# Attention scores: the negated maxima as two more rows of the queries, sent by transfers, in place of matmuls that pick them

## The chip, the cores and the metric

The kernel runs on one core of one Trainium2 chip. The metric is device microseconds for one execution; a time is the median of some runs of the same program. PE is TensorE, PEld its weight loads, DVE VectorE, ACT ScalarE, POOL GpSimd, and SP the engine that issues most transfers (its queue is SPq in the trace).

## What is computed

A gray edge filter turns 8 images of 256 x 256 into 8 sequences of 256 rows by 256 features; then come an attention block of 16 heads of 16 features and a feed-forward block. Cut to what matters here:

```
h = edges(gray(x))                                     # (8, 256, 256)
q, k, v = (layernorm(h) @ W + b for each), q and k folded with Wp
scores = einsum('bnhi,bmhi->bnhm', q, k) / sqrt(D)     # D = 16
attn = softmax(scores, axis=-1)                        # exp(scores - max over m)
h = h + einsum('bnhm,bmhe->bnhe', attn, v)
h = h + 0.5 * feed-forward-like block of layernorm(h)
```

The step of interest is the subtraction of each query's maximum before the exponential.

## The kernel before

**Stages.** Four pairs of images pass through the edge filter, the normalisation and the query, key and value products (until about 102 us). Queries and keys are split into a high and a low part of their fp32 value, written to DRAM by `store_qk` and read back by `load_qk` in another layout: `qs` and `ks` hold, for each unit of two heads, 48 rows (three terms of 16 features) on partitions 0 to 47 for the first head and 64 to 111 for the second. Then comes attention (102 to 213 us), then the feed-forward block.

**Attention.** One step `s` (64 steps: 8 images, 8 units of two heads each) makes the scores of two heads of one image. The loop at the end of the TensorE program runs in rounds of two steps: `scores_by_query(s+10)` (L1209), `scores_by_key(s)` and `scores_by_key(s+1)` (L1232 and L1237), `scores_by_query(s+11)`, then `attend` (L1257), which multiplies finished exponentials with the values for four heads.

- `scores_by_query(k)`: four matmuls, scores with queries on the partitions, two banks of one ring of three banks. DVE's `largest` (L848) takes the negated maxima from them, one reduction per head, which frees the bank (semaphore `ring_freed`). It runs 10 steps ahead of the scores that use the maxima.
- After each four steps POOL splits the four units' maxima into a high and a low part (`split_max`), `neg` (L1267) transposes them into a bank of the same ring, and ACT copies them to `negrow` (`neg_rows`, L1054). `out` (L1275) transposes finished attention through the same ring; DVE scales it (L856, L859).
- `scores_by_key(s)`: the scores again, with keys on the partitions, in the banks `p2`. Since the maximum now lies along the free dimension, it is put into the bank first: two matmuls of 512 columns (L1232), whose stationary operand `pick` is a column of zeros and ones, spread one unit's row of `negrow` over all 128 partitions, and the four score matmuls (L1237) add to it. ACT's `exp_head` (L1047) then takes the exponentials.

**Where one waits.** `scores_by_key(0)` waits for `s_neg` (ACT has copied `negrow`), every fourth step likewise, and all steps wait for the exponentials two steps back. SP's program is one list in order: the stores of the last pair are issued by `store_qk(3, i)`, behind 24 loads of the pair before, and are followed by the loads of the feed-forward weights (`load_ffn`, L401 and L404).

The lines which the change turns on:

```
if u % 4 == 0:
    wait_drained(eng, ("neg", b, u // 4))
...
eng.matmul(p2[(n + v) % 4]..., pick[rows, u % 4:u % 4 + 1].broadcast_to([SPLIT, P]),
           negrow[rows, u // 4]..., start=True, stop=False)
```

Of the kernel before, what the change touches and what calls it, by code (L numbers as in the profile page):

```python
# [5 lines left out]
def vit_tower_kernel(nc, x, scharr, Wq, bq, Wk, bk, Wv, bv, Wp, ln_gamma, ln_beta,  # L6
# [13 lines left out]
    P = 128  # L20
# [15 lines left out]
    NCOL = HALF + SPLIT  # L36
# [46 lines left out]
    pick = at("pick", 18.5, [P, 4], fp32r)  # L83
    picked = at("picked", 18.5625, [P, 4], fp32)
    negrow = at("negrow", 18.75, [NCOL, 2, N], fp32r)
# [4 lines left out]
    negsplit = at("negsplit", 24.125, [P, NT, NCOL], fp32)  # L90
# [71 lines left out]
    with ctx:  # L162
# [22 lines left out]
        s_pick = sem("pick_ready")  # L185
# [183 lines left out]
        def _(eng):  # L369
# [20 lines left out]

            def stored(p, m):
                for i in (2 * m, 2 * m + 1):
                    eng.wait_ge(s_store[i], 32 * (p + 1))
# [27 lines left out]
            eng.dma_start(b2[:], fc2_bias.rearrange("(a n) -> a n", a=1).broadcast_to([P, E])).then_inc(s_small, 16)  # L421
            for b in range(4, B):
                load_x(b)
# [24 lines left out]
            for i in range(4):  # L448
                store_qk(3, i)

# [6 lines left out]
            for s in range(SLOTS):  # L457
                for p in (2, 3):
                    first = UNITS * (2 * p - 3) + 4
                    for m in range(KE):  # L460
                        k = s - first - 4 * m
                        if 0 <= k < 4:
                            if k == 0:
                                stored(p, m)
                            eng.wait_ge(s_p2, max(s, UNITS * (2 * p - 3) + 4 * (m + 1)))
                            for i in range(3 * k, 3 * k + 3):
                                load_qk(p, m, i)
                if s in (19, 20):
                    if s == 19:
                        eng.wait_ge(s_w1f, 2)  # L470
                    eng.wait_ge(s_p2, s)
                    load_ffn(1, 2 * s - 38)
                    load_ffn(1, 2 * s - 37)
# [10 lines left out]
        def _(eng):  # L484
# [35 lines left out]
            link(eng.memset(negsplit[:], 0.0))  # L520
# [24 lines left out]
            def split_max(b, half):  # L545
# [5 lines left out]
                hi, lo = ([negsplit[:, :, HALF * v + 4 * part:HALF * v + 4 * part + 4] for v in range(2)] for part in range(2))  # L551
# [138 lines left out]
        def _(eng):  # L690
# [66 lines left out]

            eng.wait_ge(s_ident, 1)
            link(eng.tensor_reduce(picked[:], ident[:].rearrange("p (v c r u) -> p u v c r", v=2, c=8, r=2)[:, :, :, 0], AX.XY, ALU.add))
            eng.tensor_copy(pick[:], picked[:]).then_inc(s_pick, 1)  # L760
# [219 lines left out]
        def _(eng):  # L980
# [68 lines left out]
            def neg_rows(b, half):  # L1049
                key = ("neg", b, half)  # L1050
                wait_entry(eng, key)
                if b >= 1:
                    eng.wait_ge(s_p2, UNITS * (b - 1) + 4 * (half + 1))
                eng.activation(negrow[:, half], entry_bank(key)[0:NCOL, 0:N], ACT.Copy).then_inc(s_neg, 1)  # L1054

# [79 lines left out]
        def _(eng):  # L1135
# [78 lines left out]
            def scores_by_key(s):  # L1214
# [3 lines left out]
                if s == 0:  # L1218
                    eng.wait_ge(s_pick, 1)

                    wait_drained(eng, [key for key in entries[:in_a] if ebank[key] == 3][-1])
                if u % 4 == 0:
                    wait_drained(eng, ("neg", b, u // 4))
# [6 lines left out]
                for v in range(2):  # L1230
                    rows = slice(HALF * v, HALF * v + SPLIT)
                    eng.matmul(p2[(n + v) % 4][:, :].rearrange("p (t n) -> p t n", t=NT), pick[rows, u % 4:u % 4 + 1].broadcast_to([SPLIT, P]),  # L1232
                               negrow[rows, u // 4].unsqueeze(1).broadcast_to([SPLIT, NT, N]), start=True, stop=False)
                for t in range(NT):
                    for v in range(2):
                        rows = slice(HALF * v, HALF * v + SPLIT)
                        ins = eng.matmul(p2[(n + v) % 4][:, t * N:(t + 1) * N], ks[rows, r, u, c + t * P:c + (t + 1) * P],  # L1237
                                         qs[rows, r, u, c:c + N], start=False, stop=t == NT - 1)
                ins.then_inc(s_p2, 1)

            def attend(G, t):
                b, g = G // 4, G % 4
                if t == 0:
# [4 lines left out]
                    if G == 0:  # L1248
                        eng.wait_ge(s_zero, 4)
# [12 lines left out]
            def neg(b, half):  # L1262
# [3 lines left out]
                for t in range(NT):  # L1266
                    ins = eng.transpose(entry_bank(key)[0:NCOL, t * P:(t + 1) * P], negsplit[:, t], ident[:])  # L1267
# [164 lines left out]
```

## Time and profile before

| | |
|---|---|
| median of 3 runs | 308.85 us (308.3 to 309.14) |
| profiled execution | 308.78 us, its span 307.0 us |
| PE busy | 286.5 us of the span |
| PEld, DVE, ACT, POOL busy | 224.3, 213.6, 161.4, 132.1 us |
| exponentials (L1047) | 128 of 602 ns |
| maxima (L848) | 128 of 684 ns |
| picking matmuls (L1232) | 128 of 398 ns, in pairs beside each other |
| transfers | 35.30 MB, mean 115 GB/s |

The span is the time from the first to the last instruction; 1.78 us of the profiled execution lie around it. A matmul's duration in the trace includes its way through the array, so that matmuls overlap: what one costs is the distance of the starts.

### The profile page before, as it was taken

What the parts mean: (1) busy time and instruction counts of PE and PEld (TensorE: products, weight loads), DVE (VectorE), ACT (ScalarE), POOL (GpSimd) and SP (SyncE); (2) the same over time, 40 slices, a digit from 0 to 9 for tenths busy, and PEclk for the clock granted to TensorE, in tenths of its full rate; (3) what the DMA queues carried; (4) which work ended last, traced back from release to release, by engine and by line L of the source; (5) the groups of instructions that cost most, each with busy time, mean ns of one, the idle gap of its engine ahead of it and who ended that gap; (6) DMA issues with size and microseconds to landing.
All of it is one profiled execution on the core that took longest, in us unless ns stands there. A gap on an engine that the chain in (4) does not pass through costs nothing.

```text
span 307.0 us, 6170 instructions
## 1 busy us (share of the span) xinstructions
PE 286.5 (93%) x2280; PEld 224.3 (73%) x2280; DVE 213.6 (70%) x423; ACT 161.4 (53%) x304; POOL 132.1 (43%) x250
## 2 busy tenths in 40 slices
PE   0499999999999999999999999898999999999996
PEld 0378878887677766666666666565898988989976
DVE  8978984785799988888889888634835734642332
ACT  1391453523333478768777876776344434434440
POOL 7605240330200018862859562066759489500000
DMA  6978019895398971678582000000000200200202
GB/s 211 324 191 270 2 69 288 181 217 206 108 281 252 326 270 55 183 185 270 162 174 76 4 3 2 0 2 2 0 1 2 69 2 0 68 2 0 70 0 68
DMA packets 26631, 35.30 MB, mean 115 GB/s; under 512 B 5082, under 2 KB 15594, under 8 KB 26602
## 3 DMA queue, kind: packets, MB, share of 16 engines
q1 hardware_dynamic: 26440, 34.77, 38.0%
q8 instruction: 18, 0.29, 0.4%
q10 hardware_dynamic: 162, 0.15, 0.1%
q14 instruction: 11, 0.09, 0.1%
HBM read 24.42 MB, written 10.49 MB: 114 GB/s over the span
## 4 chain that ended last, share of the span: by engine, by line
PE 81%; DVE 13%; ACT 3%; issue 2%; ACTq 0%; DVEq 0%
PE bank L1139 46%; PE bank L1257 9%; PE bank L1209 8%; PE bank L1232 4%; PE bank L1237 4%; DVE negmax L848 3%; PE bank L1275 3%; PE bank L1267 1%; DVE gray L725 1%; PE bank L1161 1%; PE bank L1283 1%; PE bank L1176 1%; DVE qk_l L838 1%; DVE gray L724 1%; DVE xn L813 1%
## 5 line engine op out<-in xcount | busy, mean ns | idle before, releaser
L848 DVE TENSOR_REDUCE negmax<-bank 128x2 f32<-128x512 f32 x128 | 82.0, 684 | 6.1 <-PE bank L1209 5.8
L1047 ACT ACTIVATE probs<-bank 128x512 f32<-128x512 f32 x128 | 66.1, 602 | 28.2 <-PE bank L1237 28.2
L902 DVE TENSOR_TENSOR y_l<-yf,y_h 128x512 fp32r<-128x512 f32 x32 | 23.7, 743 | 39.1 <-ACT yf L1073 39.0
L1070 ACT ACTIVATE y_h<-bank,b1col 128x512 fp32r<-128x512 f32 x32 | 22.1, 689 | 47.8 <-PE bank L1139 47.8
L1139 PE MATMUL bank<-w_h,y_h 128*128 128x256 f32 x128 | 36.9, 289 | 2.5 <-DVE y_l L902 2.1
L1139 PE MATMUL bank<-w_h,y_l 128*128 128x256 f32 x128 | 36.2, 282 | 0.0
L1139 PE MATMUL bank<-w_l,y_h 128*128 128x256 f32 x128 | 36.2, 282 | 0.0
L1257 PE MATMUL bank<-probs,vals 128*32 128x256 f32 x512 | 34.3, 385 | 0.0
L1209 PE MATMUL bank<-ks,qs 48*128 48x256 f32 x256 | 32.2, 329 | 1.3 <-DVE negmax L848 0.7
L1209 PEld LDWEIGHTS bank<-ks,qs 48*128 48x128 f32 x256 | 19.3, 184 | 15.7 <-DVE negmax L848 6.4
L1139 PEld LDWEIGHTS bank<-w_h,y_h 128*128 128x128 f32 x128 | 24.4, 190 | 4.6 <-DVE y_l L902 3.6
L1237 PEld LDWEIGHTS bank<-qs,ks 48*128 48x128 f32 x256 | 24.2, 184 | 2.7
L1232 PE MATMUL bank<-negrow,pick 48*128 48x512 f32 x128 | 25.8, 398 | 0.0
L1139 PE MATMUL bank<-nt_h,w_h 128*128 128x512 f32 x64 | 25.8, 402 | 0.0
L1237 PE MATMUL bank<-qs,ks 48*128 48x256 f32 x256 | 25.5, 277 | 0.0
L1139 PE MATMUL bank<-nt_h,w_l 128*128 128x512 f32 x64 | 25.3, 395 | 0.0
L1139 PE MATMUL bank<-nt_l,w_h 128*128 128x512 f32 x64 | 25.0, 390 | 0.0
L1139 PEld LDWEIGHTS bank<-w_h,y_l 128*128 128x128 f32 x128 | 24.4, 191 | 0.7
L1139 PEld LDWEIGHTS bank<-w_l,y_h 128*128 128x128 f32 x128 | 24.4, 190 | 0.0
L1073 ACT ACTIVATE yf<-bank,b1col 128x512 f32<-128x512 f32 x32 | 21.8, 682 | 1.4 <-DVE y_l L902 1.4
L553 POOL TENSOR_SCALAR negsplit<-negmax 128x8 fp32r<-128x8 f32 x32 | 5.9, 205 | 38.4 <-DVE negmax L848 35.4
L563 POOL TENSOR_TENSOR hid<-hid,att 128x256 f32<-128x256 f32 x16 | 12.1, 757 | 23.6 <-DVE att L859 23.5
(147 smaller groups left out, 612.6 us busy)
## 6 DMA issues: line engine op xcount, KB each, us to landing
xr<-in_x SPq DMA_DIRECT2D x8, 768.0 KB, 9.0
qs<-qk_parts SPq DMA_DIRECT2D x48, 128.0 KB, 3.3
ks<-qk_parts SPq DMA_DIRECT2D x48, 128.0 KB, 3.4
qk_parts<-qk_h SPq DMA_DIRECT2D x16, 256.0 KB, 3.2
qk_parts<-qk_l SPq DMA_DIRECT2D x16, 256.0 KB, 3.5
wraw<-in_L_ffn_fc_q SPq DMA_DIRECT2D x4, 512.0 KB, 4.6
wscale<-in_L_ffn_fc_scales SPq DMA_DIRECT2D x4, 512.0 KB, 6.7
out<-osb SPq DMA_DIRECT2D x16, 128.0 KB, 1.8
```

The source lines that it names most:

```text
L563: eng.tensor_tensor(h, h, att[:, u % 2, :], ALU.add).then_inc(s_h2, 1)
L848: eng.tensor_reduce(negmax[:, b % 2, u, v], entry_bank(key)[:, :].rearrange("p (t k) -> p t k", t=NT), AX.X, ALU.max, negate=True).then_in ...
L902: eng.tensor_tensor(y_l[:, p % 2, f], yf[:, n % 2], y_h[:, p % 2, f].bitcast(fp32), ALU.subtract).then_inc(s_y, 1)
L1047: eng.activation(probs[:, n % PBUF], p2[n % 4][:, :], ACT.Exp).then_inc(s_exp, 1)
L1070: eng.activation(y_h[:, p % 2, f], src, ACT.Silu, bias=b1col[:, f:f + 1])
L1073: eng.activation(yf[:, n % 2], src, ACT.Silu, bias=b1col[:, f:f + 1]).then_inc(s_silu, 1)
L1139: ins = eng.matmul(dst, l, r, start=first and i == 0, stop=i == len(steps) - 1 and not more_after)
L1209: ins = eng.matmul(entry_bank(("head", k, v))[:, t * N:(t + 1) * N], qs[rows, r, u, c + t * P:c + (t + 1) * P], ks[rows, r, u, c:c + N], s ...
L1232: eng.matmul(p2[(n + v) % 4][:, :].rearrange("p (t n) -> p t n", t=NT), pick[rows, u % 4:u % 4 + 1].broadcast_to([SPLIT, P]), negrow[rows, ...
L1237: ins = eng.matmul(p2[(n + v) % 4][:, t * N:(t + 1) * N], ks[rows, r, u, c + t * P:c + (t + 1) * P], qs[rows, r, u, c:c + N], start=False, ...
L1257: ins = eng.matmul(av[OROWS * j:OROWS * (j + 1), 0:N], vals[:, b, t, h * VW:h * VW + OROWS], probs[:, (4 * G + j) % PBUF, t * N:(t + 1) * ...
L1275: ins = eng.transpose(entry_bank(key)[:, g * P:(g + 1) * P], otr_of(4 * b + g)[:, t * P:(t + 1) * P], ident[:])
```

## The change

The maxima become two more rows of the contraction. `qs` gets on partitions 48 and 49 (and 112, 113) the high and the low part of the negated maxima; `ks` gets two rows of ones there. The score matmuls then contract over 50 rows and give score minus maximum by themselves, and the two picking matmuls of each step are gone. `scores_by_key` starts its bank itself.

The rows come by transfers: after ACT has copied the transposed maxima (now 16 rows in place of 112) to `negrow`, SP issues two transfers per half image (`pass_neg`), each of 2 x 4 x 256 elements, with the semaphores `neg_rows_loaded0` and `neg_rows_loaded1`; 16 half images make 32 transfers. `scores_by_key` waits for these and no longer for ACT's copy, and ACT's next copy waits for the transfers that read `negrow`. Four transfers fill the rows of ones from a small tile, in front of the loads of images 4 to 7. Two small DVE instructions that made `pick` are gone, and POOL clears a smaller tile.

```
@@ sync, helpers
+            def pass_neg(b, half):
+                wait_drained(eng, ("neg", b, half))
+                if b >= 4:
+                    eng.wait_ge(s_p2, UNITS * (b - 4) + 4 * (half + 1))
+                cols = slice((b % 2) * N, (b % 2 + 1) * N)
+                for v in range(2):
+                    row = HALF * v + SPLIT
+                    eng.dma_start(qs[row:row + 2, (b // 2) % 2, half * 4:(half + 1) * 4, cols].bitcast(fp32),
+                                  negrow[8 * v:8 * v + 8, half, :].bitcast(fp32)).then_inc(s_nld[half], 16)
@@ sync, before load_x(4)
+            eng.wait_ge(s_zero, 3)
+            for r in range(2):
+                for v in range(2):
+                    row = HALF * v + SPLIT
+                    eng.dma_start(ks[row:row + 2, r].rearrange("p u (c n) -> p (u c) n", n=P).bitcast(fp32),
+                                  ones[:].unsqueeze(1).broadcast_to([2, UNITS * COLS // P, P])).then_inc(s_ones, 16)
@@ sync, last pair
             for i in range(4):
                 store_qk(3, i)
+                if i == 1:
+                    pass_neg(0, 0)
+            pass_neg(0, 1)
@@ sync, attention
             for s in range(SLOTS):
+                if s >= 1 and neg_after(s - 1):
+                    pass_neg(*neg_after(s - 1))
@@ vector
-            eng.wait_ge(s_ident, 1)
-            link(eng.tensor_reduce(picked[:], ident[:].rearrange("p (v c r u) -> p u v c r", v=2, c=8, r=2)[:, :, :, 0], AX.XY, ALU.add))
-            eng.tensor_copy(pick[:], picked[:]).then_inc(s_pick, 1)
@@ scalar, neg_rows
                 if b >= 1:
-                    eng.wait_ge(s_p2, UNITS * (b - 1) + 4 * (half + 1))
-                eng.activation(negrow[:, half], entry_bank(key)[0:NCOL, 0:N], ACT.Copy).then_inc(s_neg, 1)
+                    eng.wait_ge(s_nld[half], 32 * b)
+                eng.activation(negrow[:, half], entry_bank(key)[0:16, 0:N], ACT.Copy).then_inc(s_neg, 1)
@@ tensor, scores_by_key
                 if s == 0:
-                    eng.wait_ge(s_pick, 1)
+                    eng.wait_ge(s_ones, 64)
...
                 if u % 4 == 0:
-                    wait_drained(eng, ("neg", b, u // 4))
+                    eng.wait_ge(s_nld[u // 4], 32 * (b + 1))
...
-                for v in range(2):
-                    rows = slice(HALF * v, HALF * v + SPLIT)
-                    eng.matmul(p2[(n + v) % 4][:, :].rearrange("p (t n) -> p t n", t=NT), pick[rows, u % 4:u % 4 + 1].broadcast_to([SPLIT, P]),
-                               negrow[rows, u // 4].unsqueeze(1).broadcast_to([SPLIT, NT, N]), start=True, stop=False)
                 for t in range(NT):
                     for v in range(2):
-                        rows = slice(HALF * v, HALF * v + SPLIT)
+                        rows = slice(HALF * v, HALF * v + KSTACK)
...
-                                         qs[rows, r, u, c:c + N], start=False, stop=t == NT - 1)
+                                         qs[rows, r, u, c:c + N], start=True, stop=True)
```

**Order on PE, the first round of attention.** Before, from `scores_by_query(10)` to `scores_by_query(11)`; the name in brackets is the semaphore waited for:

```order
L1209 MATMUL bank<-ks,qs 128x256 [waits ring_freed]
L1209 MATMUL bank<-ks,qs 128x256 x3
L1232 MATMUL bank<-negrow,pick 128x512 [waits neg_rows_copied,freed0,pick_ready]
L1232 MATMUL bank<-negrow,pick 128x512
L1237 MATMUL bank<-qs,ks 128x256 x4
L1232 MATMUL bank<-negrow,pick 128x512 [waits freed2,freed1]
L1232 MATMUL bank<-negrow,pick 128x512
L1237 MATMUL bank<-qs,ks 128x256 x4
L1209 MATMUL bank<-ks,qs 128x256 [waits ring_freed]
```

The same stretch of PE's list after the change (L1227 is the former L1209, L1251 the former L1237):

```order
L1227 MATMUL bank<-ks,qs 128x256 [waits ring_freed]
L1227 MATMUL bank<-ks,qs 128x256 x3
L1251 MATMUL bank<-qs,ks 128x256 [waits neg_rows_loaded0,freed0,neg_rows_copied,rows_of_ones_loaded]
L1251 MATMUL bank<-qs,ks 128x256 x3
L1251 MATMUL bank<-qs,ks 128x256 [waits freed2,freed1]
L1251 MATMUL bank<-qs,ks 128x256 x4
L1227 MATMUL bank<-ks,qs 128x256 [waits ring_freed]
```

The four picking matmuls are gone, and the first score matmul waits for a transfer.

**Order on SP, the end of the last pair.** Before, from the last loads of the pair before to the feed-forward weights:

```order
L389 DMA ks<-qk_parts 16x4x512 x6
L379 DMA qk_parts<-qk_h 128x512 [waits freed2]
L379 DMA qk_parts<-qk_l 128x512
L379 DMA qk_parts<-qk_h 128x512 [waits freed3]
L379 DMA qk_parts<-qk_l 128x512
L379 DMA qk_parts<-qk_h 128x512 [waits freed0]
L379 DMA qk_parts<-qk_l 128x512
L379 DMA qk_parts<-qk_h 128x512 [waits freed1]
L379 DMA qk_parts<-qk_l 128x512
L401 DMA wraw<-in_L_ffn_fc_q 128x1024 [waits qk_stored1,qk_stored0,filled2]
```

After, from the second store of that pair on:

```order
L379 DMA qk_parts<-qk_h 128x512 [waits freed3]
L379 DMA qk_parts<-qk_l 128x512
L399 DMA qs<-negrow 2x4x256 [waits neg_rows_copied]
L399 DMA qs<-negrow 2x4x256
L379 DMA qk_parts<-qk_h 128x512 [waits freed0]
L379 DMA qk_parts<-qk_l 128x512
L379 DMA qk_parts<-qk_h 128x512 [waits freed1]
L379 DMA qk_parts<-qk_l 128x512
L399 DMA qs<-negrow 2x4x256 [waits neg_rows_copied]
L399 DMA qs<-negrow 2x4x256
```

The first two transfers of maxima stand behind four stores and the next two behind all eight, in front of the feed-forward weights.

## Rows read from the trace of the kernel before

**Rows 1.** The page's chain that ended last, share of the span by line:

```profile
PE bank L1139 46%; PE bank L1257 9%; PE bank L1209 8%; PE bank L1232 4%; PE bank L1237 4%; DVE negmax L848 3%; PE bank L1275 3%; PE bank L1267 1%; DVE gray L725 1%; PE bank L1161 1%; PE bank L1283 1%; PE bank L1176 1%; DVE qk_l L838 1%; DVE gray L724 1%; DVE xn L813 1%
```

**Rows 2.** Timeline, a round: start us, us, engine, line, operation [idle before <-releaser]:

```profile
143.22 0.50 PE L1209 MATMUL bank<-ks,qs 48*128 48x256 f32 x4
143.56 0.40 PE L1232 MATMUL bank<-negrow,pick 48*128 48x512 f32 x2
143.83 0.69 DVE L848 TENSOR_REDUCE negmax<-bank 128x2 f32<-128x512 f32 x1 [0.24 <-PE bank L1209]
143.92 0.19 PEld L1232 LDWEIGHTS bank<-negrow,pick 48*128 48x128 f32 x2
144.03 0.39 PE L1232 MATMUL bank<-negrow,pick 48*128 48x512 f32 x2
144.26 0.40 PE L1237 MATMUL bank<-qs,ks 48*128 48x256 f32 x4
144.57 0.30 PEld L1209 LDWEIGHTS bank<-ks,qs 48*128 48x128 f32 x4
145.00 1.07 PE L1257 MATMUL bank<-probs,vals 128*32 128x256 f32 x16
```

**Rows 3.** Timeline, a round whose ring also carries an output:

```profile
151.34 0.40 PE L1237 MATMUL bank<-qs,ks 48*128 48x256 f32 x4
151.78 0.30 PEld L1209 LDWEIGHTS bank<-ks,qs 48*128 48x128 f32 x4 [0.25 <-DVE negmax L848]
```

**Rows 4.** An issue of SP; landing of the stores issued 101.1 and 101.6; landing of output stores:

```profile
102.10 0.73 SPq L379 DMA_DIRECT2D qk_parts<-qk_h  x1
...
DMA to landing us min/median/max: 3.2/3.4/3.6
...
out<-osb SPq DMA_DIRECT2D x16, 128.0 KB, 1.8
```

**Rows 5.** Timeline, weight loads of the first steps of attention:

```profile
102.09 0.19 PEld L1232 LDWEIGHTS bank<-negrow,pick 48*128 48x128 f32 x2
103.25 0.30 PEld L1209 LDWEIGHTS bank<-ks,qs 48*128 48x128 f32 x4 [0.15 <-DVE negmax L848]
108.10 0.19 PEld L1232 LDWEIGHTS bank<-negrow,pick 48*128 48x128 f32 x2
```

**Rows 6.** Landing of the stores issued from 104.0 to 104.7 us:

```profile
DMA to landing us min/median/max: 3.5/3.9/4.3
```

**Rows 7.** Timeline, rounds after the last maxima:

```profile
194.41 0.66 PE L1283 MATMUL bank<-ident,n 128*128 128x128 f32 x4 [0.87 <-ACT negrow L1054]
...
195.00 0.50 PE L1232 MATMUL bank<-negrow,pick 48*128 48x512 f32 x2
195.33 0.40 PE L1237 MATMUL bank<-qs,ks 48*128 48x256 f32 x4
195.77 2.07 ACT L1047 ACTIVATE probs<-bank 128x512 f32<-128x512 f32 x4 [1.41 <-PE bank L1237]
196.12 1.07 PE L1257 MATMUL bank<-probs,vals 128*32 128x256 f32 x16
197.71 0.50 PE L1232 MATMUL bank<-negrow,pick 48*128 48x512 f32 x2
```

**Rows 8.** Timeline, the start of DVE's gray sums:

```profile
8.87 0.18 DVE L759 TENSOR_REDUCE picked<-ident 128x4 f32<-128x16 f32 x1
9.16 0.87 DVE L724 SCALAR_TENSOR_TENSOR gray<-xr,gray 128x512 f32<-128x512 f32 x1
```

**Rows 9.** Landing of the images 4 to 7, issued at 17.3 to 20.5 us, and their first reader:

```profile
DMA to landing us min/median/max: 6.9/9.0/10.2
...
34.56 0.64 ACT L998 ACTIVATE gray<-xr 128x512 f32<-128x512 f32 x1
```

**Rows 10.** Chain in order of time: start us, us, work; the edge filter's first matmuls:

```profile
13.71 4.18 PE bank L1139 x9
...
21.04 2.09 PE bank L1139 x9
```

More of the change, by code:

```diff
@@ L35, in vit_tower_kernel @@
     HALF = P // 2
-    NCOL = HALF + SPLIT
+    KSTACK = SPLIT + 2
     UNITS = HEADS // 2
@@ L82, in vit_tower_kernel @@
     unused = at("unused", 18.375, [P, 1], fp32)
-    pick = at("pick", 18.5, [P, 4], fp32r)
-    picked = at("picked", 18.5625, [P, 4], fp32)
-    negrow = at("negrow", 18.75, [NCOL, 2, N], fp32r)
+    negrow = at("negrow", 18.75, [16, 2, N], fp32r)
     b2 = at("b2", 20.75, [P, E], fp32)
@@ L89, in vit_tower_kernel @@
     recip = at("recip", 24, [P, 2, HEADS], fp32)
-    negsplit = at("negsplit", 24.125, [P, NT, NCOL], fp32)
+    negsplit = at("negsplit", 24.125, [P, NT, 16], fp32)
+    ones = at("ones", 24.25, [2, P], fp32)
     vals = at("vals", 25, [P, B, NT, HEADS * VW + 16], fp32)
@@ L184, in vit_tower_kernel @@
         s_border = sem("gray_borders_zeroed")
-        s_pick = sem("pick_ready")
+        s_ones = sem("rows_of_ones_loaded")
+        s_nld = [sem("neg_rows_loaded0"), sem("neg_rows_loaded1")]
         s_band = sem("band_ready")
@@ L519, in _ @@
             link(eng.memset(mhalf[:], -0.5))
-            link(eng.memset(negsplit[:], 0.0))
+            eng.memset(ones[:], 1.0).then_inc(s_zero, 1)
             eng.memset(vals[:, :, :, 0:HEADS * VW].rearrange("p b t (h v) -> p (b t) h v", v=VW)[:, :, :, D:VW], 1.0).then_inc(s_zero, 1)
@@ L550, in split_max @@
                 src = negmax[:, b % 2, half * 4:(half + 1) * 4].rearrange("p u v t -> p v t u")
-                hi, lo = ([negsplit[:, :, HALF * v + 4 * part:HALF * v + 4 * part + 4] for v in range(2)] for part in range(2))
+                hi, lo = ([negsplit[:, :, 8 * v + 4 * part:8 * v + 4 * part + 4] for v in range(2)] for part in range(2))
                 for v in range(2):
@@ L1248, in attend @@
                     if G == 0:
-                        eng.wait_ge(s_zero, 4)
+                        eng.wait_ge(s_zero, 5)
                         wait_read(eng, last_turns[3])
@@ L1266, in neg @@
                 for t in range(NT):
-                    ins = eng.transpose(entry_bank(key)[0:NCOL, t * P:(t + 1) * P], negsplit[:, t], ident[:])
+                    ins = eng.transpose(entry_bank(key)[0:16, t * P:(t + 1) * P], negsplit[:, t], ident[:])
                 ins.then_inc(s_ent, 1)
```

## The prediction

> **What bounds the kernel now.** I read the page's busy shares first: PE is busy nearly throughout. The chain that ended last gives the line of the picking matmuls, L1232, 4% of the span, or some 12.9 us [rows 1]. The views that decide are the timelines of PE, its weight loads and DVE in single rounds, for they tell whether a pick delayed anything.
>
> Rows 2 show a round. The first query scores start at 143.22, the first pick 0.34 us later, a pick with its four score matmuls takes 0.47 (143.56 to 144.03), and `attend` starts at 145.00 and takes 1.00. DVE takes a maximum from 143.83 to 144.52, and only then is the bank free for the second query scores, whose weights are loaded at 144.57. Had they waited for nothing, that load would have stood where loads stand that are pulled ahead: 0.11 us ahead of the matmul's start (143.92 for the one of 144.03), so about 0.11 behind the last score matmul's start, at 144.37. So there were 0.20 us to spare: **DVE's first maximum, not the picks, sets the second query scores.** In a round that carries an output, DVE begins later and the spare time is larger: the load comes 0.44 behind the last score matmul's start and has DVE as its releaser [rows 3]. The rest of a round is query scores, `attend` and DVE's other maxima, none of which the change touches. After the last query scores (step 53) PE has no such wait, and a round is PE from end to end [rows 7].
>
> **The change part by part.**
>
> Picks in steps 0 to 53: two picks per step go, 0.47 − 0.24 = 0.23 us of a step, 0.46 of a round. The cover is DVE's maximum: PE reaches the second query scores 0.46 earlier and waits 0.46 longer. Gain 0. Bounds: none below 0; above, the most a round could gain is DVE's idle time of 0.24 [rows 2], 27 rounds, 6.5 us, if something that I take for DVE's pace were PE's. I take 0, since both spare times are positive.
>
> Picks in steps 54 to 63: five rounds. In rows 7 the pick starts at 195.00, the scores at 195.33, the exponentials at 195.77, `attend` at 196.12. Without picks the exponentials start 0.33 earlier and `attend` 0.46 earlier than now, counted from the round's start. The round took 2.71 (195.00 to 197.71) and would take 2.25. ACT needs for four exponentials 2.07 and for a copy of half the columns some 0.25 more (an estimate, half of one exponential's share), 2.3 in all, so it may hold back this shortest round by 0.05 to 0.1. The first of the five rounds gains only 0.33, as its end hangs on ACT: PE's next transposes, at 194.41, waited for ACT's copy of the last maxima [rows 7], which stands behind the exponentials. Sum 0.33 + 4 x 0.47 = 2.2 us, gained; bounds 1.2 (ACT sets all five, 5 x 0.23) and 2.3.
>
> The wait of step 0: now its first weight load stands at 102.09 and the second query scores of that round at 103.25 [rows 5]. Afterwards it needs the first two transfers. SP comes to them when it now issues the next store, at 102.10 [rows 4]; an issue takes about 0.5, so the second goes out at 102.6. In front of them are the stores issued at 101.1 and 101.6, which land after 3.2 and 3.6, the later at 105.2 [rows 4]. On quiet queues a transfer lands 1.8 after its issue [rows 4], which would be 104.4. I take 105.1, near the store, because these queues are full, with 104.4 and 106.9 (4.3 after issue, like the slowest in rows 6) as bounds. Then the scores load weights at 105.15; the second step follows 0.23 behind, and the second query scores at 105.15 + 0.11 + 0.23 + 0.11 = 105.6, against 103.25: a shift of **2.4 us**. It reaches everything behind, since PE waits in order and the maxima behind that stand in DVE's queue have no other work to fill the hole. Bounds 1.7 and 4.2.
>
> The wait of step 4: its weights load at 108.10 [rows 5], with the shift at 110.5. The second pair of transfers goes out behind the last two stores, which now issue at 104.0 and 104.7 and land within 4.3 [rows 6], the last at 109.0. With four more issues ahead the pair lands at 109.8 to 110.6. A delay of up to 0.66 there (0.20 + 0.46) is swallowed by the next wait for DVE. I take 0; if it lands like the slowest store it costs up to 1.
>
> Later transfers have two rounds, at least 2 x 2.78 = 5.6 us (a round of rows 2 goes from 143.22 to the end of `attend` at 146.00) [rows 2], for a copy that is read by SP, two issues and a landing of 3 to 4 [rows 4, 6]; the one for image 1 stands behind the feed-forward weights and has least to spare. I take 0. SP's own list grows by 32 issues of about 0.5, among loads that wait for PE's steps anyway.
>
> The rows of ones: four issues on SP and 256 KB in front of images 4 to 7. Those land 9.0 after issue, at most 10.2, so by 30.7, and the first is read at 34.56, when it had landed at about 24 [rows 9]. The ten microseconds between cover the four transfers. Cost 0.
>
> DVE's two instructions: 9.16 − 8.87 = 0.29 us in front of the gray sums [rows 8], which are the chain until PE begins. I take 0.25, gained, bounds 0 and 0.3.
>
> The two added rows (50 in place of 48) and 16 in place of 112 transposed rows: the number of columns streamed is the same. Within 0.1 either way.
>
> Sum: −0.25 + 2.4 − 2.2 = −0.05 us. The profiled execution took 308.78, the median is 308.85; the forecast on the scale of the median is **308.8 us**.
>
> The page "DMA: Bandwidth & Descriptors" of the Trainium skill, in "Why a DMA increments its semaphore by 16 and not by 1", says that a transfer is split over as many engines as divide both outermost dimensions. By it the 2 x 4 x 256 transfers would use two of sixteen, and land when those two have done with their part of the stores; no row here shows which two, so the bounds above stand.
>
> **The rivals.**
>
> *A longer hole, or a lower clock behind it (slower).* PE stands still from about 102.3 to 105.15. At the kernel's start nine matmuls took 4.18 us, later ones 2.09: the clock was at its lower level (1.2 GHz against 2.4) behind the idle start [rows 10]. If the hole brings it back for two to three rounds, their matmuls stretch from 2.23 us in a round (0.34 + 0.46 + 0.43 + 1.00) by a factor of 4.18 / 2.09 = 2 at most, to 3.5 if `attend` is bound by something else and to 4.5 if not, against 2.78 now, which costs 0.7 to 1.7 a round, so 1.4 to 5 us. It decides from the point where the hole is long enough to lower the clock; I price it at 2.3, near the lower end, since DVE's pace hides the first part. Without the clock, transfers that land like the slowest store make the hole 1.8 longer. Time: 308.8 + 2.3 = 311.1. The Trainium skill, "TensorE: Matmul & The Clock Gate", "HAM oscillation — how this bites in real kernels", warns that waits between bursts of matmuls return the array to its low clock; no row before the change has a hole like this one.
>
> *The transfers land soon (faster).* At 104.4 the shift is 1.7, the sum −0.75; with the picks gaining also a little beside the negated maxima's copy, −1.3: 307.5.
>
> *The picks were on the path in every round (faster).* The chain says so with 12.9 us. Against it stand the spare times. DVE's idle time limits it: −6.5, so 302.
>
> **How the numbers follow.** About 0.3% (0.9 us) is what a measurement can tell from no change. Forecast of balance, 0.50, its own range 307.9 to 309.8, of which 0.04 fall on either side beyond 0.3%; longer hole or lower clock 0.30; soon landed 0.14, of which 0.02 stay within; picks on the path 0.06. That gives faster 0.22, same 0.44, slower 0.34. Leaving out a tenth at each end, the range is 307.2 to 311.4.
>
> **What would show it.** Right: PE's first `scores_by_key` waits for a transfer for about 3 us at 102; rounds in the middle take as long as before, the one like rows 2 2.78 us; PE's weight loads of the second query scores now have DVE as releaser in nearly each round; the last five rounds are 2.2 us shorter; the feed-forward block starts where it did. Wrong: rounds shorter by some tenths; a second hole at step 4 or 8; score matmuls with starts twice as far apart behind the hole.

## The result, and the profile after

The changed kernel is slower: 320.04 us (317.92 to 322.93, 4 runs) against 308.87 (308.3 to 309.14, 4 runs), a ratio of 1.034, 95% interval 1.029 to 1.040. The forecast was 308.8 with 311.4 as its upper end, so the loss of 11.2 us lies far outside. Where the ratio of an experiment stands below beside its median, it leaves out executions in which the records show a longer spell at the lower clock.

The profiled execution took 317.92 us, its span is 316.2 us, 9.2 more than before. It was the fastest of the four; the others took 1.6 to 5.0 us more and have no trace, so the account below covers 9.2 us of the 11.2 between the medians. The page of the changed kernel, its row of the granted clock (40 slices of 7.9 us) and the head of its chain that ended last:

```profile
PEclk9999999999999599998799999999999999999999
...
PE 65%; DVE 21%; SPq 5%; issue 3%; DMA 3%; ACT 2%; ACTq 0%; DVEq 0%
PE bank L1157 42%; DVE negmax L866 8%; PE bank L1271 7%; PE bank L1227 6%; SPq L389 4%; DMA qs<-negrow 3%; PE bank L1251 3%; PE bank L1289 2%; DVE qk_l L856 2%; DVE gray L747 1%; PE bank L1179 1%; PE bank L1297 1%; DVE xn L831 1%; SPq L399 1%; DVE att L877 1%
```

Before, the clock stood at 9 in all 40 slices and neither SP nor a transfer of maxima was in the chain [rows 1]. Now the clock drops in two places, and SP's issues have 5% of the chain: the loads L389 4%, the new transfers L399 1%. The waits of PE by what ended them, then those of SP (us in total, times, longest):

```profile
PE bank L1227 <- DVE negmax L866: 9.8, 23, 0.7
PE bank L1251 <- DMA qs<-negrow: 9.4, 3, 5.3
...
SPq L399 <- ACT negrow L1072: 42.7, 9, 8.5
```

The first row answers to the spare time of [rows 2, 3]: PE now waits 0.7 at most for DVE, 23 times; that is where the picks' time went. The second row is where the loss begins: three waits for a transfer, 9.4 us, each with a price behind it. The third is SP, an engine with a list of its own, standing still in front of the new transfers, up to 8.5 us, with everything behind them in that list.

**The first wait (step 0).** Timeline, SP, PE's weight load and matmuls at the start of attention:

```profile
101.39 0.50 PE L1227 MATMUL bank<-ks,qs 48*128 48x256 f32 x4 [0.44 <-DVE negmax L866]
101.89 1.82 SPq L399 DMA_DIRECT2D qs<-negrow  x2
105.20 0.96 PEld L1251 LDWEIGHTS bank<-qs,ks 50*128 50x128 f32 x8 [3.52 <-issue]
105.23 1.01 PE L1251 MATMUL bank<-qs,ks 50*128 50x256 f32 x6 [3.34 <-DMA qs<-negrow]
```

Against [rows 5] (102.09) the weights load at 105.20. The clock of that stretch, from the windows (busy us and count by engine, then PEclk, DMA share, GB/s):

```profile
100.00:105.00 5.00, 1.46 (x13) 1.05 (x11) 3.29 (x7) 0.00 (x0) 0.00 (x0) 0.85 0.95 292
105.00:110.00 5.00, 4.77 (x32) 4.24 (x32) 1.75 (x3) 2.09 (x5) 0.72 (x4) 0.50 0.90 302
110.00:115.00 5.00, 4.54 (x58) 2.42 (x56) 4.33 (x8) 4.55 (x10) 0.00 (x0) 0.96 0.92 272
```

0.50 is the level of 1.2 GHz. DVE's maxima, compared by their starts in the two traces, stood 0.47 us earlier than before ahead of this place and 4.33 later behind it: a shift of 4.8 us.

**The second wait (step 24), not foreseen.** SP's issues around it, with ACT's copy that the pair of 145.60 sends, and PE's weight load and matmuls:

```profile
124.26 0.37 ACT L1072 ACTIVATE negrow<-bank 16x256 fp32r<-16x256 f32 x1
124.66 1.26 SPq L399 DMA_DIRECT2D qs<-negrow  x2
...
126.04 3.81 SPq L389 DMA_DIRECT2D qs<-qk_parts  x6
...
129.89 4.62 SPq L389 DMA_DIRECT2D ks<-qk_parts  x6
...
134.55 1.36 SPq L399 DMA_DIRECT2D qs<-negrow  x2
...
136.03 3.79 SPq L389 DMA_DIRECT2D qs<-qk_parts  x6
137.46 0.37 ACT L1072 ACTIVATE negrow<-bank 16x256 fp32r<-16x256 f32 x1
...
139.86 4.52 SPq L389 DMA_DIRECT2D ks<-qk_parts  x6
...
144.48 1.08 SPq L412 DMA_DIRECT2D wraw<-in_L_ffn_fc_q  x2
...
145.60 1.36 SPq L399 DMA_DIRECT2D qs<-negrow  x2
...
150.42 1.22 PE L1251 MATMUL bank<-qs,ks 50*128 50x256 f32 x8 [5.26 <-DMA qs<-negrow]
```

The same queue in the kernel before, from the first loads of image pair 2 to the weights of the second layer:

```profile
118.25 4.99 SPq L389 DMA_DIRECT2D qs<-qk_parts  x6
...
123.28 4.58 SPq L389 DMA_DIRECT2D ks<-qk_parts  x6
...
127.97 3.75 SPq L389 DMA_DIRECT2D qs<-qk_parts  x6
131.76 3.79 SPq L389 DMA_DIRECT2D ks<-qk_parts  x6
135.65 1.82 SPq L401 DMA_DIRECT2D wraw<-in_L_ffn_fc_q  x2
```

Read from below: the maxima for step 24 lay in `negrow` at 137.83, but SP sent them only at 145.60. From 126.04 to 144.38 it issues without a gap over 0.15: 24 loads in 16.7 us, 0.70 each, and one pair of transfers. With the first wait's shift alone the loads would have begun at 118.25 + 4.3 = 122.6; they begin at 126.04, because the pair in front of them (124.66) waits for ACT's copy of 124.26. So SP starts 3.4 late and has no slack to catch up. Then 1 MB of weights goes out at 144.48, one place ahead of the pair, which lands only at 150.4. DVE's maxima shift from 4.23 to 10.93 here: 6.7 us. The clock is low again:

```profile
148.00:154.00 6.00, 3.58 (x30) 2.08 (x30) 1.29 (x2) 2.07 (x5) 0.43 (x3) 0.50 0.73 248
154.00:160.00 6.00, 5.30 (x62) 3.66 (x66) 4.74 (x9) 4.50 (x10) 2.64 (x5) 0.94 0.01 3
```

**The third (step 40)** is short, PE waits 0.79 us, the shift grows by 0.4. **The tail** (steps 54 to 63) gives 2.0 back: the shift is 11.15 at the last maxima and the spans differ by 9.2. In sum −0.47 + 4.80 + 6.70 + 0.40 = 11.43, less 0.28 of small drifts 11.15, and 11.15 − 1.95 = 9.2.

### The profile page after: what moved, and what is told of

It reads as the page before. It is cut to its first block, busy times and chain, and to the rows that moved or that the text cites. A ratio compares the mean times of both kernels' runs of the same rounds, so it can differ in the third digit from the quotient of the medians.

```text
span 316.2 us, 5956 instructions
## 1 busy us (share of the span) xinstructions
PE 277.1 (88%) x2152; PEld 214.1 (68%) x2152; DVE 213.2 (67%) x421; ACT 162.5 (51%) x304; POOL 131.6 (42%) x250
## 4 chain that ended last, share of the span: by engine, by line
PE 65%; DVE 21%; SPq 5%; issue 3%; DMA 3%; ACT 2%; ACTq 0%; DVEq 0%
PE bank L1157 42%; DVE negmax L866 8%; PE bank L1271 7%; PE bank L1227 6%; SPq L389 4%; DMA qs<-negrow 3%; PE bank L1251 3%; PE bank L1289 2%; DVE qk_l L856 2%; DVE gray L747 1%; PE bank L1179 1%; PE bank L1297 1%; DVE xn L831 1%; SPq L399 1%; DVE att L877 1%
## 5 line engine op out<-in xcount | busy, mean ns | idle before, releaser
L1227 PE MATMUL bank<-ks,qs 48*128 48x256 f32 x256 | 33.0, 336 | 10.6 <-DVE negmax L866 9.8
L1227 PEld LDWEIGHTS bank<-ks,qs 48*128 48x128 f32 x256 | 20.2, 193 | 26.8 <-DVE negmax L866 16.4
L1271 PE MATMUL bank<-probs,vals 128*32 128x256 f32 x512 | 35.1, 393 | 0.0
L1251 PE MATMUL bank<-qs,ks 50*128 50x256 f32 x256 | 23.2, 301 | 9.4 <-DMA qs<-negrow 9.4
L1251 PEld LDWEIGHTS bank<-qs,ks 50*128 50x128 f32 x256 | 19.0, 201 | 11.5 <-DMA qs<-negrow 6.5
L1157 PE MATMUL bank<-gray_h,band_h 128*128 128x512 f32 x48 | 20.4, 425 | 0.7 <-DVE gray_l L752 0.7
```

The costliest lines, as they stand in the source:

```text
L1157: ins = eng.matmul(dst, l, r, start=first and i == 0, stop=i == len(steps) - 1 and not more_after)
L1227: ins = eng.matmul(entry_bank(("head", k, v))[:, t * N:(t + 1) * N], qs[rows, r, u, c + t * P:c + (t + 1) * P], ks[rows, r, u, c:c + N], s ...
L1271: ins = eng.matmul(av[OROWS * j:OROWS * (j + 1), 0:N], vals[:, b, t, h * VW:h * VW + OROWS], probs[:, (4 * G + j) % PBUF, t * N:(t + 1) * ...
```

## The experiments

Eleven kernels ran beside the two, one of them timed twice; all are below. "Shift" is how much later the maxima (or exponentials) of a step start than in the trace before. Experiments 2 to 6 and 8 are one execution each. The four of the changed kernel spread over 5 us, so these six are read from their traces, and their times are no more than a rough check.

**1. The picks taken out and nothing put in their place.**

```
-                for v in range(2):
-                    eng.matmul(p2[...], pick[...], negrow[...], start=True, stop=False)
...
-    ACT.Exp)
+    ACT.Exp, scale=0.01)
```

> The kernel before without its 128 picking matmuls, and nothing sent in their place: the maxima are still found, split, transposed and copied, but not subtracted (the exponential is taken of 0.01 times the score, at the same cost), so this part of the computation is left out. Theory 'the picks were hidden by DVE in steps 0 to 53': the exponentials of steps 0 to 52 start within 0.5 us of where they did, only the last five rounds gain, time 2.0 to 2.5 us under before, about 306.6. Rival 'the picks were on the path in every round', as the chain has it: 6 to 13 us under before. Rival 'a PE with less to do gets the lower clock': granted clock under 1.0 somewhere in attention, and no gain.

Measured: 306.77 us against 309.17, ratio 0.993 (0.991 to 0.996). In the trace the exponentials of steps 12 to 54 all keep one shift (−0.86 to −0.90, from an earlier start); it goes to −2.32 by step 62 and −2.5 in the span. PE's waits:

```profile
PE bank L1209 <- DVE negmax L848: 11.7, 28, 0.7
```

28 waits against 2 of 0.7 us in all before. So the picks of steps 0 to 53 were worth nothing and those of the tail 1.6 us (from −0.9 to −2.5); the change had no more than some 2 us to win. The granted clock stayed at 1.00, so the rival of a lower clock is out.

**2. The hole of step 0 in the kernel before.** PE also waits at step 0 until the second of the last pair's four stores (`s_store[1]`) has landed; no maxima are sent.

```
                     eng.wait_ge(s_pick, 1)
+                    eng.wait_ge(s_store[1], 32 * PAIRS)
```

> The kernel before with one wait added: PE's step 0 waits until the second half's key store of pair 3 has landed, near 105.2. Nothing else changes; it is the hole by itself. Theory 'a hole of 3 us lowers the clock for a while': granted clock 0.5 from about 103 to 110, step 2's exponentials 4.0 to 4.5 us later than before's, time 4 us over before. Rival 'the clock falls only together with the missing picks': clock 1.0, step 2 is 3 us late, time 3 us over.

Measured: 313.08 us, span 311.3. Timeline and windows:

```profile
104.25 0.80 PE L1233 MATMUL bank<-negrow,pick 48*128 48x512 f32 x2 [2.38 <-issue]
```

```profile
100.00:105.00 5.00, 2.20 (x16) 1.76 (x17) 3.25 (x7) 0.00 (x0) 0.00 (x0) 0.80 0.97 352
105.00:110.00 5.00, 5.00 (x36) 4.28 (x34) 1.88 (x3) 2.07 (x4) 0.72 (x4) 0.51 1.00 312
```

The shift goes from −0.50 to +4.32 and stays there to the end. A wait of 2.4 us at this place costs 4.8, with no transfer of maxima anywhere: about half of the price is what follows the hole, in which the granted clock is 0.51.

**3. The hole filled.** The changed kernel with 24 idle transposes on PE where it waits.

```
                 if s == 0:
+                    wait_read(eng, last_turns[3])
+                    keep_busy(24)
```

> The changed kernel with 24 idle transposes of the identity on PE (0.11 us each, 2.6 us) between the first query scores of attention and the wait of step 0. The hole is as long, but PE is busy in most of it. Theory 'the clock fell because PE stood still there, and that cost about 1.0 us': the granted clock stays at 1.0 until step 24, step 2's exponentials start 3.2 us after before's and not 4.2. Rival 'the clock fell for another reason': it falls as before and step 2 stays 4.2 late, or later by what the transposes take.

Measured: 317.38 us. PE at the hole, and a window behind it:

```profile
101.62 2.84 PE L1184 MATMUL bank<-ident 128*128 128x128 f32 x24 [0.29 <-DVE vals L849]
...
105.00:110.00 5.00, 4.89 (x56) 3.17 (x56) 3.86 (x6) 4.57 (x10) 0.72 (x4) 1.00 0.86 303
```

The clock is 1.00 from 100 to 115. The score matmuls start at 104.77, as long after the query scores in front of them as in the changed kernel (3.9 against 3.8), and the shift is 3.0 (−1.03 to +2.00) in place of 4.8: **the lower clock behind the first hole costs 1.8 us.** The hole at step 24 stays, 5.2 us.

**4. The first pair sent ahead of the loads of the pair before.**

```
             stored(1, 1)
+            pass_neg(0, 0)
             for k in range(12):
                 load_qk(1, 1, k)
...
-                if i == 1:
-                    pass_neg(0, 0)
```

> The changed kernel with the first two transfers of maxima issued in front of the 12 loads of pair 1's second half (near 92 us) instead of behind the second store of pair 3. Theory 'the hole at step 0 is SP's order and costs 3.2 us and 1.0 more by the clock': step 0's exponentials start at about 102.5, step 2's at most 3 us later, everything behind is 4.2 us earlier until step 22, and the hole at step 24 stays. Rival 'the rows of ones or something else holds step 0': no change at step 0. Rival 'the second pair of transfers takes over': a hole of 1 us or more at step 4.

Measured: 320.38 us. No hole at step 0 (shift −0.60), but at step 4, where PE waits 2.1 us for the second pair, and step 24 keeps 5.7 us. The place in SP's list makes the hole; moving one pair only uncovers the next, as the last rival said.

**5. The weights of the second layer two steps later.**

```
-                if s in (19, 20):
+                if s in (21, 22):
```

> The changed kernel with the second layer's weights loaded after steps 21 and 22 in place of 19 and 20, so that no megabyte stands in front of the maxima for step 24. Theory 'two causes for the hole at step 24, SP's late arrival and the weights in front': SP still issues these transfers near 144, they land about 3 us later, near 147, and the hole shrinks from 5.3 to 2 to 3 us; the low clock behind it is gone or shorter; time 3 to 4 us under the changed kernel. Rival 'only the weights in front': the hole goes wholly, 6 to 7 us under. Rival 'only SP's arrival': the hole stays at 5.

Measured: 322.69 us, a miss as a whole. Two parts of it lie away from step 24. Up to step 20 this is the changed kernel's own list, yet the first hole costs 6.6 us here in place of 4.8: the wait is 3.7 in place of 3.3, and the lower clock lasts until 114.7, 10.2 us in place of 6.8. The same kernel's hole thus has no fixed price, which may be a part of why its executions differ by 5 us; no trace shows the others. And the wait at step 40 grew from 0.8 to 1.8. At step 24 it tells what was asked:

```profile
147.09 1.35 SPq L399 DMA_DIRECT2D qs<-negrow  x2
148.55 0.93 SPq L412 DMA_DIRECT2D wraw<-in_L_ffn_fc_q  x2
...
149.75 1.22 PE L1251 MATMUL bank<-qs,ks 50*128 50x256 f32 x8 [2.41 <-DMA qs<-negrow]
```

Without the weights in front, the pair lands 2.7 us after its first issue in place of 4.8, and PE waits 2.4 in place of 5.3. It is still issued 7 us after ACT's copy (139.66). Two causes, then: SP's lateness, and 1 MB ahead. The lower clock behind the hole stayed, against the expectation (10.2 us of it, against 6.8 in the changed kernel).

**6. Only the pair for step 24 moved**, from SP to ACT, behind its copy.

```
-                if s >= 1 and neg_after(s - 1):
+                if s >= 1 and neg_after(s - 1) and s != 20:
...
+                if (b, half) == (3, 0):
+                    wait_drained(eng, key)
...
+                    for v in range(2):
+                        eng.dma_start(qs[...], negrow[...]).then_inc(s_nld[half], 16)
```

> The changed kernel with one thing moved: the two transfers of image 3's first half, which step 24 reads, are issued by ACT behind its copy in place of SP. If the hole at step 24 comes from their place in SP's list: the hole is gone, the lower clock behind it too, the shift of step 24 stays at that of step 22 (within 0.7), and the time is 320.0 - 6.5 = 313.5 (312.3 to 314.5). The hole at step 0 stays, about 4.8 with its clock. Rival, they are late because the queues are full with weights wherever they are issued: the hole stays at 3 to 5 us, with a time of 317 to 320. Second rival, the next half (step 28), which stands in SP's list behind the same weights, takes the hole over: shift of 2 to 4 at step 28, 315.5 to 318.

Measured: 314.2 us, span 312.5. At step 24 the shift stays at 4.08 (exponentials). But the next pair takes the hole over, for step 28:

```profile
137.94 1.41 ACTq L1080 DMA_DIRECT2D qs<-negrow  x2
...
144.61 1.08 SPq L412 DMA_DIRECT2D wraw<-in_L_ffn_fc_q  x2
...
146.75 5.64 SPq L399 DMA_DIRECT2D qs<-negrow  x4
...
153.90 0.73 PE L1260 MATMUL bank<-qs,ks 50*128 50x256 f32 x8 [2.23 <-DMA qs<-negrow]
```

The shift there is 3.2, as the second rival said; the time is that of the first answer. By spans 3.7 is gained, and 6.7 + 0.4 − 3.2 = 3.9, since the short wait at step 40 went too. The transfers moved to ACT were in time with the queues as full as ever, so it was SP's list that held them.

**7. SP's list put in an order by hand**: both pairs of image 0 ahead of the loads, later pairs behind the loads of their step, the weights two steps later.

```
             stored(1, 1)
+            pass_neg(0, 0)
             for k in range(12):
                 load_qk(1, 1, k)
+            pass_neg(0, 1)
...
-                if s >= 1 and neg_after(s - 1):
-                    pass_neg(*neg_after(s - 1))
                 for p in (2, 3):
...
+                if s >= 1 and neg_after(s - 1):
+                    pass_neg(*neg_after(s - 1))
-                if s in (19, 20):
+                if s in (21, 22):
```

> The changed kernel, transfers still on SP, with three moves in SP's list: the first pair of transfers in front of the 12 loads of pair 1's second half, the second pair behind them and in front of the stores of pair 3, the later ones behind the three loads of the same step instead of in front, and the second layer's weights after steps 21 and 22. Theory 'only the order in SP's list costs': holes at steps 0 and 4 are gone, SP comes to the transfers for step 24 some 5 us earlier than in the changed kernel (near 138 to 140) and that hole is under 1 us, the clock stays at 1.0; time 306.5 to 308. Rival 'SP is short of issue time in any order, 24 loads of 0.6 us in 8 steps of 1.65': a hole of 2 us or more at step 20 or 24 remains and the clock falls once; time 311 to 315.

Measured: 312.96 us, ratio 1.014 (1.009 to 1.019). No hole at steps 0 and 4; one at step 8, behind the weights of the first layer:

```profile
110.85 4.42 SPq L399 DMA_DIRECT2D qs<-negrow  x4
...
117.86 1.22 PE L1250 MATMUL bank<-qs,ks 50*128 50x256 f32 x8 [3.73 <-DMA qs<-negrow]
```

Its shift is 7.0 (−0.28 to +6.70), and two short waits near steps 28 and 32 add another 1.1. The time is the rival's (311 to 315). Within one list I found no order without a hole, of the three that were tried (4, 5 and 7).

**8. The transfers sent but not waited for.** The kernel before, picks and all, with the 32 transfers in SP's list; only ACT's next copy waits for them.

```
             for s in range(SLOTS):
+                if s >= 1 and neg_after(s - 1):
+                    pass_neg(*neg_after(s - 1))
...
                     eng.wait_ge(s_p2, UNITS * (b - 1) + 4 * (half + 1))
+                    eng.wait_ge(s_nld[half], 32 * b)
```

> The kernel before, picks and all, with the 32 transfers of maxima issued by SP at the places where the changed kernel issues them, into the two free rows, but PE not waiting for them (ACT's next copy does). Theory 'the transfers themselves cost nothing, PE's wait for them does': time within 1 us of before, PE's rounds as before, while SP issues the second layer's weights near 142 instead of 135.65. Rival 'the traffic or SP's lateness costs by itself': time over before by 2 us or more.

Measured: 310.31 us, clock 1.0 throughout. The shift goes from −0.69 to +0.85 at step 12 and to +1.53 at step 32. The weights of the second layer go out at 140.74 in place of 135.65, though PE hardly moved, and POOL, which unpacks weights and splits maxima in one list, is late:

```profile
PE bank L1287 <- POOL negsplit L573: 2.3, 2, 1.5
```

These two waits are the 2.2 us of shift, by way of POOL. The second (0.8) follows from the late SP: POOL starts on the second layer's weights at 149.36 in place of 145.50. For the first (1.5 us, at 120.39) that is not shown: POOL waited there for the first layer's weights (4.3 us against 2.5 before), but it also waits 4.0 and 5.5 us for them in experiment 9, where SP sends no maxima.

**9. All transfers from ACT's queue**, each pair right behind its copy. Timed twice.

```
-                if s >= 1 and neg_after(s - 1):
-                    pass_neg(*neg_after(s - 1))
...
                 eng.activation(negrow[:, half], entry_bank(key)[0:16, 0:N], ACT.Copy).then_inc(s_neg, 1)
+                wait_drained(eng, key)
...
+                for v in range(2):
+                    eng.dma_start(qs[...], negrow[...]).then_inc(s_nld[half], 16)
```

> The changed kernel with all 32 transfers of maxima issued by ACT on its own queue, right behind its copy, and none by SP. Theory 'SP's list is the cause of both holes': no wait of PE for these transfers above 0.5 us, granted clock 1.0 throughout, all rounds as long as before, last five rounds 2.2 shorter, time 2 to 2.5 us under before, about 306.7. Rival 'a transfer through DRAM-side traffic is late from any queue': holes of 1 us or more at step 24 and at step 4 remain, time over before. Rival 'ACT becomes the bound, since each issue takes about 0.6 us of it': exponentials wait, rounds with a copy are 0.5 to 1 us longer, 16 of them, time 3 to 10 us over that of the kernel without picks.

Measured: 306.79 us against 308.49, ratio 0.995 (0.989 to 1.001).

> The changed kernel with all 32 transfers sent by ACT, both right behind its copy: the same kernel as the earlier one, timed again in five rounds beside the spread one, since its interval reached to no change. Expected is the ratio of then, 0.995 (0.993 to 0.998), so about 307. If ACT's issues ahead of the exponentials are what it gives away against the spread one, it is 0.5 to 1 us slower than that one; if not, the two agree within 0.3.

Measured: 307.98 us (306.53 to 311.8, 12 runs) against 308.68, ratio 0.998 (0.995 to 1.001). PE's waits in the first of the two:

```profile
PE bank L1254 <- ACT probs L1060: 2.2, 6, 0.5
...
PE bank L1254 <- DMA qs<-negrow: 1.0, 1, 1.0
```

The loss is gone, and neither interval shows a gain. What is left in this trace are six waits for exponentials, which now start behind ACT's two issues (1.3 us), and one short wait at step 8. The trace of the second timing (309.8 us) has one thing more, PE's wait for POOL at 120.27 and what POOL had waited for:

```profile
PE bank L1284 <- POOL negsplit L573: 2.4, 1, 2.4
...
115.48 1.04 POOL L627 TENSOR_SCALAR w1full<-wraw 128x1024 f32<-128x1024 int32 x1 [5.51 <-DMA wscale<-in_L_ffn_fc_scales]
```

The first layer's weights landed late, POOL, which splits maxima behind them in its list, with them, and the clock was at its lower level from 120.9 to 127.7. The shift goes from −1.7 to +2.7 there. So a hole can still open with the transfers on ACT, by another way.

**10. ACT's two issues spread over two steps**, each behind that step's exponentials.

```
+                if s >= 1 and neg_after(s - 1):
+                    send_neg(*neg_after(s - 1), 0)
...
+                if s >= 2 and neg_after(s - 2):
+                    send_neg(*neg_after(s - 2), 1)
```

> The changed kernel, but ACT sends the 32 transfers, and not both at once: the first of a half image goes out one step after ACT's copy, behind that step's exponentials, the second one step later. If what is lost in the changed kernel is only the place of the transfers in SP's list, and what the run with both behind the copy gave away is ACT's issue time ahead of the exponentials: PE waits for a transfer for less than 1 us in all, clock at the upper level throughout, no shift of DVE's maxima by more than 0.5 us until step 53, the tail's 2 us kept, so about 308.5 - 2.2 = 306.3 on the median (range 305.8 to 307). Rival, the transfers themselves are what costs (ports or queues, wherever they are issued): as with both behind the copy or longer, 306.8 to 308.5, with PE's waits for a transfer of 2 us and more.

Measured: 307.74 us (305.53 to 311.56, 6 runs) against 308.68, ratio 0.993 (0.990 to 0.995). The waits for exponentials are gone; transfers are late at steps 8 and 24, the first of them with the lower clock behind it:

```profile
PE bank L1264 <- DMA qs<-negrow: 2.7, 2, 1.6
...
107.59 0.63 ACTq L1076 DMA_DIRECT2D qs<-negrow  x1
...
109.74 0.63 ACTq L1076 DMA_DIRECT2D qs<-negrow  x1
...
114.91 0.74 PE L1264 MATMUL bank<-qs,ks 50*128 50x256 f32 x8 [1.57 <-DMA qs<-negrow]
...
115.81 1.93 PE L1284 MATMUL bank<-probs,vals 128*32 128x256 f32 x16
```

`attend` takes 1.93 there in place of 1.07: the clock. The median missed the 306.3 that I expected and is level with experiment 9's; time and waits (2.7 us in all) are those that the rival named. The ratio says 0.7% less than before, the median of all six executions 0.3%, and the lower clock is what a late transfer brings this kernel in its own trace; so a gain of the whole kernel is not shown.

**11. The pair for step 8 one step sooner.**

```
-                    send_neg(*neg_after(s - 1), 0)
+                    send_neg(*neg_after(s - 1), neg_after(s - 1) == (1, 0))
...
+                if neg_after(s) == (1, 0):
+                    send_neg(1, 0, 0)
```

> The spread kernel with one half image earlier: the transfers of image 1's first half, which step 8 reads, go out behind ACT's copy and one step later, in place of one and two steps later. In the spread kernel that pair was issued at 107.59 and 109.74, behind 2 MB of feed-forward weights, PE waited 1.57 us for it at 114.9, and the clock was at its lower level for 3.4 us behind it. If issue time decides: the pair goes out at 107.2 and 107.8 to 108.3, lands about 1.5 us sooner, PE's wait is under 0.5, the clock stays up, and the profiled run is 2 to 3 us shorter than the spread one's 308.5: 306 for it, and a median of 306.3 (305.5 to 307.2), ratio about 0.992. Rival, the weights in front decide and not the issue: they land when the 2 MB have landed, the wait stays at 1.3 to 1.6, and the median at 307 to 308.

Measured: 307.97 us (305.83 to 313.27, 7 runs) against 308.64, ratio 0.996 (0.992 to 0.999).

```profile
107.91 0.63 ACTq L1076 DMA_DIRECT2D qs<-negrow  x1
108.03 0.91 SPq L415 DMA_DIRECT2D wscale<-in_L_ffn_fc_scales  x2
...
108.63 0.63 ACTq L1076 DMA_DIRECT2D qs<-negrow  x1
...
115.14 0.74 PE L1266 MATMUL bank<-qs,ks 50*128 50x256 f32 x8 [1.07 <-DMA qs<-negrow]
```

PE's wait fell from 1.57 to 1.07 us, between what was expected (under 0.5) and what the rival said (1.3 to 1.6). With the second issue 1.1 us sooner, and SP's weights 0.4 later, PE waited 0.5 less, and 6.5 us still lie between the second issue and PE's start. The view of the DMA queues tells where they go: from 108.0 to 112.7 it has packets of SP's queue only, and all 20 packets of ACT's two transfers run between 112.7 and 115.0. The transfers waited 4.9 us for their first packet, while SP's 2 MB were moved; the last of these landed at 115.65. The weights decide most of the landing, as the rival had it, and the issue time a little. The Trainium skill, "DMA: Bandwidth & Descriptors", "Queues, rings and completion order", says that SP and ACT have rows of their own and each DMA engine goes round between the rows with work, by packets, which would let a small transfer of ACT overtake SP's weights. This trace agrees only in part: the transfers were done 0.5 us ahead of the last weights (2.3 us ahead in the second trace of experiment 9), but for the first 4.9 us none of their packets ran, and no run shows why.

Together experiments 9 to 11 have 30 executions. In 20 the mean granted clock is 0.999 or more; they take 305.5 to 308.3 us, with a median of 306.7, which is 2 us under before, the worth of the tail. The other 10, with a mean clock of 0.977 to 0.994, take 308.5 to 313.3 and use it up. Two of these have a trace, and both show a hole of PE with the lower clock behind it (experiment 10 and the second of 9); for the other eight that is not shown.

## Why the prediction was wrong

- **The step that failed** is the term for the later transfers: "I take 0. SP's own list grows by 32 issues of about 0.5, among loads that wait for PE's steps anyway." The loads do wait for PE's steps, but they are 24 in 8 steps at 0.6 to 0.8 us each, so SP was busy nearly without a break from 118.25 to 137.5 in the kernel before. A transfer of maxima took 0.6 to 1.1 to issue, not 0.5. I had not looked at this stretch of SP's timeline. Thirty-two more issues, and above all a wait for ACT in front of such a block, move everything behind by microseconds; the two rounds of time that I granted each transfer were counted from ACT's copy and not from when SP would come to it. Cost 6.7 + 0.4 us. Experiment 6 removes it at step 24 by moving two transfers only (a smaller hole then opens at step 28), 5 splits it in two causes, 9 removes it altogether.
- **Transfers stand behind weights.** I named this for image 1 (step 8), where it cost nothing with SP's queue as changed, and overlooked the other 2 MB at steps 19 and 20, where it added about 2 us.
- **Step 0: the hole was right, its price was not.** The weights load at 105.20 (predicted 105.15). That the two agree so well is partly luck: the two issues took 1.8 us and not 1.0, and in other traces of the same list the weights load at 104.74 (experiment 3), 105.97 (5) and 105.23 (6). The shift is 4.8 in place of 2.4. Of the 2.4 too much, 1.8 is the lower clock (experiment 3); the rest is near the 0.47 us by which PE arrived earlier than before at the same landing. The rival of the lower clock had this, with 1.4 to 5 and a price of 2.3, and I gave it 0.30 and left it out of the sum; the clock fell in each profiled execution in which the hole stood unfilled at step 0. The doubling of matmul times at the start of the kernel, from which the rival took its price, has no granted clock beside it (the record gives 1.00 for 2 to 14 us); behind the holes both are on record. Without steps 24 and 40 the kernel would still have been slower, by the trace some 311 (308.8 − 0.5 + 4.8 − 2.0), by the medians some 313 (320.0 − 6.7 − 0.4).
- **Step 4** cost nothing in the changed kernel, as predicted, but behind a hole that had made PE late anyway: where that hole is gone (experiment 4), PE waits 2.1 us for the second pair.
- **Picks in steps 0 to 53:** right, 0 (experiment 1, and PE's 9.8 us of waits for DVE).
- **The tail:** −2.2 predicted, −2.0 measured between the last maxima and the end, −1.9 by the same measure with the picks alone removed.
- **DVE's two instructions:** its gray sums start at 9.08 against 9.16 [rows 8], 0.1 in place of 0.25; in the other traces the same start lies between 8.92 and 9.48, so the term can't be told from the spread. **Rows of ones:** no wait for them shows.

## What to carry to other kernels

A transfer put into an engine's issue list costs at two places: it waits there for its data with everything behind it, and it is late by all that stands in front. Before adding any, read the issuing engine's timeline over the whole stretch and ask where it is busy without a break. Here the engine that makes the data was the better issuer. And a hole of 2 us or more on PE has to be priced with the clock that follows it, here 1.3 to 2 times its length in all.

## What the runs showed of the hardware

- **An issue is not cheap.** The small transfers took 0.61 to 1.09 us each to issue on SP (the changed kernel) and 0.63 to 0.90 on ACT (experiment 9, nearly all 0.63), a load L389 0.63 to 0.83 on average over six; I had taken 0.5.
- **Holes and the clock.** The records show the lower clock behind waits of PE of 3.3 and 5.3 us (the changed kernel), 2.4 (experiment 2), 2.1 (4), 2.2 (6), 3.7 (7) and 2.4 (9, second trace). Near 1.5 us it went both ways: at the lower level behind one of 1.57 (experiment 10), at the upper level behind one of 1.51 (experiment 8); behind 1.07 (experiment 11) it stayed up. Filled with idle transposes, the hole of 3 us did not bring it. The lower level lasted from 3.4 us (experiment 10) over 6.8 (both holes of the changed kernel) to 10.2 (experiment 7).
- **A landing follows the megabytes in front of it:** PE had its 8 KB transfers 4.8 us after the first issue behind 1 MB (step 24), and 6.5 us after the second beside 2 MB from another queue (experiment 11), against 2.7 after the first with nothing large ahead (experiment 5).
